# Expert stages of a two-layer block: order of the shared tile, output banks, routing by batch

## The reference

```python
# layer one: 8 experts, hidden width 128, and one shared expert without weight
scores = sigmoid(h @ gate_w.T); sel = top_k(scores + bias, 2)
routed += (silu((s*h) @ w1[e].T) * ((s*h) @ w3[e].T)) @ w2[e].T   # s: the chosen score
shared = (silu(h @ sw1.T) * (h @ sw3.T)) @ sw2.T
# layer two: 8 experts, hidden width 176, and one shared expert
p = softmax(h @ w_router); the two largest, divided by their sum, are the weights
out = sum_e weight_e * (silu(h @ w1[e]) @ w2[e]) + silu(h @ w_shared1) @ w_shared2
```

## Time and profile before

| what | value |
|---|---|
| median of 3 runs | 999.11 us |
| lowest and highest | 995.98 and 1001.66 us |
| the profiled execution | 992.07 us, of which the span is 990.3 us |
| mean granted PE clock in it | 0.939 of full |
| PE, DVE, ACT, POOL busy | 85%, 79%, 56%, 47% of the span |
| experts of layer one | about 618 to 725 us |
| heads of layer two | about 723 to 883 us |
| experts of layer two | about 889 to 985 us, the store behind it |

### The profile page before, as it was taken

The page is one execution under the profiler, slowest core; times in us unless marked ns, Lnnn a source line. Parts: engine busy times, 40 slices in busy tenths (PEclk is TensorE's granted clock), DMA queues, the critical chain, the costliest instruction groups (busy, mean ns, idle before and its releaser), DMA issues. The chain is left out here.

```text
span 990.3 us, 16625 instructions
## 1 busy us (share of the span) xinstructions
PE 844.1 (85%) x5407; PEld 596.8 (60%) x5486; DVE 780.0 (79%) x1734; ACT 553.9 (56%) x1222; POOL 466.5 (47%) x459
## 2 busy tenths in 40 slices
PE   5778899999999999999998899696966766847996
PEld 3456677767777777777776677353545424335564
DVE  6978999999999999999889997574689778583322
ACT  3758878777777877777766674011134552612111
POOL 2137676667776654554444445252222230602842
PEclk9979999999999999999999999799977887977898
DMA  7023333344333322214222223301115031022322
GB/s 255 27 65 106 135 113 105 125 133 134 112 133 127 94 85 83 79 65 128 87 86 65 86 65 141 131 23 65 47 47 89 1 51 16 1 91 74 113 68 73
DMA packets 52613, 87.15 MB, mean 88 GB/s; under 512 B 5784, under 2 KB 23704, under 8 KB 51760
## 3 DMA queue, kind: packets, MB, share of 16 engines
q1 hardware_dynamic: 43312, 73.50, 25.0%
q10 hardware_dynamic: 9216, 12.59, 3.4%
HBM read 70.67 MB, written 15.40 MB: 87 GB/s over the span
## 5 line engine op out<-in xcount | busy, mean ns | idle before, releaser
L580 PE MATMUL bank<-hTs,wA 128*128 128x512 bf16 x711 | 168.2, 382 | 3.7 <-DVE u L1813 0.5
L2343 POOL TENSOR_TENSOR xbuf<-xbuf,dec 128x384 f32<-128x384 f32 x64 | 53.5, 835 | 211.7 <-ACT xbuf L1294 169.6
L1813 DVE SCALAR_TENSOR_TENSOR u<-bank,chn,u 128x511 f32<-128x511 f32 (+2 forms) x192 | 142.9, 744 | 3.5
L580 PEld LDWEIGHTS bank<-hTs,wA 128*128 128x128 bf16 x768 | 75.5, 99 | 83.3 <-issue 4.8
L652 PE MATMUL bank<-wB,yb 128*128 128x256 f32 x512 | 121.1, 380 | 0.7 <-DVE acc L1769 0.7
L2425 POOL TENSOR_TENSOR hf<-hf 128x512 bf16<-128x512 f32 x44 | 47.5, 1080 | 116.6 <-DVE hf L2051 105.1
L580 PE MATMUL bank<-hTs,w 128*128 128x512 bf16 x354 | 89.9, 399 | 11.9 <-issue 9.4
L652 PEld LDWEIGHTS bank<-wB,yb 128*128 128x128 f32 x512 | 92.5, 190 | 11.1 <-issue 1.1
L2353 POOL TENSOR_TENSOR yb<-yv,gs 128x512 f32<-128x512 f32 x64 | 81.8, 1279 | 14.0 <-DVE yv L1840 13.8
L731 PE MATMUL bank<-Mm,xbuf 128*128 128x128 f32 x512 | 71.9, 285 | 18.8 <-DVE yv L1840 17.5
L731 PEld LDWEIGHTS bank<-Mm,xbuf 128*128 128x128 f32 x512 | 66.0, 196 | 30.2 <-issue 21.3
(11 more groups left out here) (258 smaller groups left out, 1826.1 us busy)
## 6 DMA issues: line engine op xcount, KB each, us to landing
csb<-csd SPq DMA_DIRECT2D x64, 256.0 KB, 3.5
wA<-in_win SPq DMA_DIRECT2D x32, 256.0 KB, 4.3
wAd<-wA ACTq DMA_DIRECT2D x32, 256.0 KB, 4.5
wA<-wAd SPq DMA_DIRECT2D x32, 256.0 KB, 3.8
sS<-cbd SPq DMA_DIRECT2D x24, 256.0 KB, 3.2
wB<-in_wob SPq DMA_DIRECT2D x8, 512.0 KB, 6.1
wBd<-wB ACTq DMA_DIRECT2D x32, 128.0 KB, 4.4
wB<-wBd SPq DMA_DIRECT2D x8, 512.0 KB, 5.4
```

The lines of the kernel that those rows point to most:

```text
L580: last = nc.tensor.matmul(out, wpart(a, kt), hpart(c, kt), start=n == 0, stop=n == 5)
L1813: nc.vector.scalar_tensor_tensor(out=u[:, n % 2, d:S], in0=bank[0][:, 0:S - d], scalar=chn[:, hid, 3 - d:4 - d], in1=u[:, n % 2, d:S], op0 ...
L2343: nc.gpsimd.tensor_tensor(Xw[:, n % 2, :].rearrange("p (t n) -> p t n", n=P), Xdt[:, n % 2, 0:S - P].rearrange("p (t n) -> p t n", n=P), d ...
```

## The change

- **Shared tile first.** In layer one, when tile m is shared, DVE does `hidden(m)` before `scaled(m + 1)` (at m = 0 also `gated_rows(1)` before it).
- **Turned weights and the copy.** For batch 0 of layer one PE turns the weights before `products(0)`, ACT copies them before its first `hidden`. SP issues `weight_rows(0, 0)` before the modulation weights. The pieces of work for batch 1 on PE, ACT and DVE move back by one step; the normalised rows are split from the roots and follow one step later.
- **Own output banks.** `OUT = ((6, 7), (4, 5))`: batch 0 adds up in banks 6 and 7, batch 1 in banks 4 and 5. The wait for `xf_done` goes.
- **Order of layer two.** Both shared tiles of batch 0 and then both of batch 1 come first, then batch 0's routed tiles, then batch 1's.
- **Routing by batch.** In layer two transposing, routing, split, exponent, normalising and choosing are done for batch 0, then for batch 1; the weights are turned after product 0 and after step 3. The clearing of `zerob` stands before the normalising.
- **End.** The wait for `a_x` goes. Batch 1's rows of layer two are gated and added in two halves; the store is three transfers, of batch 0 and of each half of batch 1.

The semaphores `d_wm0`, `d_wmr` and `d_wm1` become one, `d_wm`, and the early returns for `stop` go.

```diff
+        OUT = ((6, 7), (4, 5))
+        TILES = ([(b, pos) for b in range(B) for pos in range(FT[0])],
+                 [(b, pos) for b in range(B) for pos in range(SHARED[1])]
+                 + [(b, pos) for b in range(B) for pos in range(SHARED[1], FT[1])])
...
@@ SP
             sp.wait_ge(q["out_done"], TB * (N // HG))
+            weight_rows(0, 0)
             for kt in range(KT):
-                sp.dma_start(wm1[kt], io["wmod"][1, :, kt, :]).then_inc(q["d_wm1"], 16)
-            for b in range(B):
-                weight_rows(0, b, b + 1)
+                sp.dma_start(wm1[kt], io["wmod"][1, :, kt, :]).then_inc(q["d_wm"], 16)
+            weight_rows(0, 1)
...
-            weight_rows(1, 0, B)
-            sp.wait_ge(q["xf_done"], 2 * B)
-            store()
+            for b in range(B):
+                weight_rows(1, b)
+            sp.wait_ge(q["xf_done"], B + 1)
+            store(0, TB)
+            for half in range(2):
+                sp.wait_ge(q["xf_done"], B + 2 + half)
+                store(TB + 2 * half, TB + 2 * half + 2)
+            sp.wait_ge(q["d_out"], 48)
@@ PE, experts(L)
                 if L:
-                    transposed_rows(n0)
                     for b in range(B):
-                        routes(L, b, bank[6][:, b * TB * E:(b + 1) * TB * E])
+                        for ft in range(KT):
+                            turned_rows(n0, b, ft, bank[(2, 0)[b] + ft])
+                        routes(L, b, bank[4][:, b * TB * E:(b + 1) * TB * E])
...
-                pe.wait_ge(q["hts_done"], 6 if L == 0 else 12)
-                products(0)
                 if L == 0:
                     turned_weights(0, 0, bank[3])
+                    pe.wait_ge(q["hts_done"], 6)
+                    products(0)
                     pe.wait_ge(q["rg_step"], ROOT * (N // HG - 1) + 1)
                     out_product(TB - 1, N // HG - 1, bank[DRAIN[TB - 1]])
                     pe.wait_ge(q["cbT_done"], 1)
                 else:
-                    pe.wait_ge(q["rt_dve"], 1)
+                    pe.wait_ge(q["hts_done"], 10)
+                    products(0)
+                    turned_weights(1, 0, bank[1])
                 products(1)
...
-                        if m:
-                            pe.wait_ge(q["xf_done"], L * B + m // nf)
-                        for o in (6, 7):
+                        if L == 0 and b == 1:
+                            pe.wait_ge(q["cbT_done"], 2)
+                        if L and b == 1:
+                            pe.wait_ge(q["rt_dve"], 2)
+                        cleared(b)
                     rows_out(m)
-                    if L and m == 1:
-                        for b in range(B):
-                            turned_weights(1, b, bank[4 + b])
+                    if L and m == 3:
+                        turned_weights(1, 1, bank[3])
@@ DVE, experts(L)
                 else:
+                    nc.vector.memset(zerob[:], 0.0).then_inc(q["zb_done"], 1)
                     normalise(1, B)
...
+                    for b in range(B):
+                        less_largest(b)
+                        for ft in range(KT):
+                            split_part(n0, b, ft)
+                        shares(b)
...
                 for m in range(B * nf):
-                    if L == 0 and m + 1 < B * nf and tile(0, m + 1)[1] >= SHARED[0]:
+                    ahead = L == 0 and m + 1 < B * nf and tile(0, m + 1)[1] >= SHARED[0]
+                    shared = tile(L, m)[1] < SHARED[L]
+                    if ahead and not shared:
                         scaled(m + 1)
                     if L == 0:
                         first_batch(m)
                     hidden(m)
+                    if L == 0 and m == 0:
+                        gated_rows(1)
+                    if ahead and shared:
+                        scaled(m + 1)
                     if L == 0:
                         second_batch(m)
-                    if m > nf and m % nf == 1:
-                        add_experts(m // nf - 1)
-                add_experts(B - 1)
+                    if m == last_tile(L, 0) + 2:
+                        add_experts(0)
+                add_experts(1)
```

More of the change, by code:

```diff
@@ L284, in weighted @@
         def weighted(L, m):
-            b, pos, _ = tile(L, m)
-            return (B * (FT[0] - SHARED[0]) if L else 0) + b * (FT[L] - SHARED[L]) + max(0, pos + 1 - SHARED[L])
+            routed = sum(pos >= SHARED[L] for _, pos in TILES[L][:m + 1])
+            return (B * (FT[0] - SHARED[0]) if L else 0) + routed
         def hidden_tiles(L, m):
@@ L298, in spans @@
                     for e in range(E) if e * HID1 < (f + 1) * P and (e + 1) * HID1 > f * P]
-        weighted_tiles = [(L, m) for L in range(2) for m in range(B * FT[L]) if m % FT[L] >= SHARED[L]]
+        weighted_tiles = [(L, m) for L in range(2) for m in range(B * FT[L]) if TILES[L][m][1] >= SHARED[L]]
         def landed(j):
@@ L865, in experts @@
                 for m in range(B * nf):
+                    b, pos, _ = tile(L, m)
                     if m + 2 < B * nf:
-                        if L == 0 and m + 2 == nf:
-                            pe.wait_ge(q["hts_done"], 8)
+                        if tile(L, m + 2)[0:2] == (1, 0):
+                            pe.wait_ge(q["hts_done"], 8 if L == 0 else 12)
                         products(m + 2)
@@ L999, in heads @@
                 keys_queries(1)
-                pe.wait_ge(q["d_wm1"], 16 * KT)
+                pe.wait_ge(q["d_wm"], 32 + 16 * KT)
                 pe.wait_ge(q["scb_done"], 2)
@@ L2053, in add_experts, with gated, added @@
                 def add_experts(b):
-                    dve.wait_ge(q["fout"], tiles(L, nf * (b + 1) - 1))
-                    for m in range(2):
-                        last = nc.vector.tensor_tensor(xo[:, 2 * m:2 * m + 2, :],
-                                                       bank[6 + m][:, :].rearrange("p (t d) -> p t d", t=2),
+                    dve.wait_ge(q["fout"], tiles(L, last_tile(L, b)))
+                    def gated(m):
+                        return nc.vector.tensor_tensor(xo[:, 2 * m:2 * m + 2, :],
+                                                       bank[OUT[b][m]][:, :].rearrange("p (t d) -> p t d", t=2),
                                                        gm[:, L, 1, b, :].unsqueeze(1).to_broadcast([P, 2, D]), ALU.mult)
-                    link(last)
-                    part = slice(b * TB, (b + 1) * TB)
-                    nc.vector.tensor_tensor(x_sb[:, part, :], x_sb[:, part, :], xo[:], ALU.add).then_inc(q["xf_done"], 1)
+                    def added(t0, t1):
+                        part = slice(b * TB + t0, b * TB + t1)
+                        nc.vector.tensor_tensor(x_sb[:, part, :], x_sb[:, part, :], xo[:, t0:t1], ALU.add)\
+                            .then_inc(q["xf_done"], 1)
+                    if L and b:
+                        for m in range(2):
+                            link(gated(m))
+                            added(2 * m, 2 * m + 2)
+                        return
+                    gated(0)
+                    link(gated(1))
+                    added(0, TB)
                     dve.wait_ge(q["xf_done"], L * B + b + 1)
                 for m in range(B * nf):
-                    if L == 0 and m + 1 < B * nf and tile(0, m + 1)[1] >= SHARED[0]:
+                    ahead = L == 0 and m + 1 < B * nf and tile(0, m + 1)[1] >= SHARED[0]
+                    shared = tile(L, m)[1] < SHARED[L]
+                    if ahead and not shared:
                         scaled(m + 1)
@@ L2397, in low_halves, with input_rows @@
                 nf, own = FT[L], FT[L] - SHARED[L]
-                def input_rows(m):
-                    f = tile(L, m)[2]
-                    if m < SHARED[L]:
+                def input_rows(pos):
+                    f = (own + pos) % nf
+                    if pos < SHARED[L]:
                         pool.wait_ge(q["d_wa"], 32 * (L + 1))
@@ L2409, in input_rows, with output_rows @@
                         .then_inc(q["fw_done"], 1)
-                def output_rows(m):
-                    f = tile(L, m)[2]
-                    if m >= SHARED[L]:
+                def output_rows(pos):
+                    f = (own + pos) % nf
+                    if pos >= SHARED[L]:
                         pool.wait_ge(q["d_w2"], 32 * (L + 1))
@@ L2426, in hidden_rows @@
                         .then_inc(q["fhs_done"], 1)
-                for m in range(3):
-                    input_rows(m)
+                for pos in range(3):
+                    input_rows(pos)
                 for m in range(B * nf):
-                    if m < nf:
-                        output_rows(m)
+                    b, pos, _ = tile(L, m)
+                    if b == 0:
+                        output_rows(pos)
                     hidden_rows(m)
-                    if m + 3 < nf:
-                        input_rows(m + 3)
+                    if b == 0 and pos + 3 < nf:
```

(1 more changed line is left out.)

154 lines of the change are left out of this document (74 added, 80 removed).

## The result

The changed kernel takes 963.96 us (median of 4 runs, 961.88 to 964.57) against 997.88 us for the kernel before (4 runs, 995.98 to 1001.66): ratio 0.965, 95% interval 0.962 to 0.969. The forecast was 967, in 957 to 979.

A forecast was written before the change was run, and what follows sets the result against it. TensorE, the fullest engine, was taken as the bound, losing where it stands still or runs at lower clock. Gains 17.6 + 13.3 + 1.6 = 32.5 us, off the 999.11 median: 966.6, said as 967, range 957 to 979.

The forecast's parts named there:

- Layer one, opening and batch 0: Layer one's experts before the batch change: no idleness before product 2, rows out 2 at 640.4 against 650.45.
- Rival A: Layer one's batch 0: DVE becomes the bound, layer one gives 11 us, time 973 us; chance 0.17.
- Rival B: Layer one's opening: rows come no sooner, the copy's 5.5 us being its own; time 972 us; chance 0.07.
- Rival C: Layer two: the clock stays at 0.50; 1033 us if over all of it; chance 0.03.
- D: Better than forecast: clock stays up before layer two's batch 1 (16.5), roots take 2.2 us (18.6): 962 us; chance 0.13.
- Heads: The heads between the two layers' experts: only their start moves; 0, within 2 us each way.
- Batch change: Layer one, batch 0 to 1: 4.81 us of idleness for x_sb and about 1.5 us of half clock go.
- Layer two: Layer two's experts: less routing before product 0, no stall, no batch-change idleness; 13.3 us gained, 11 to 16.5.
- Tail: After the last update: a last store of 256 KB instead of 1 MB gains 1.6 us; 0 to 2.4.

The follow-up runs named there:

- changed_again: The changed kernel, unaltered, timed and profiled a second time: 960.47 us, ratio 0.964.
- one_bank_pair: The changed kernel with layer one's batch 1 adding up in banks 6 and 7 again, with PE's wait for x_sb: 966.79 us, 0.968.
- last_tile_and_rows_later: last_tile_first plus, at layer one's opening, batch 1's statistics and eight root steps one step later and cbT's copy before SP's wait: 962.63 us, 0.967.
- weights_before_copy: The changed kernel with SP issuing the modulation weights ahead of the copy of cbT and the rows again: 963.12 us, 0.967.
- batch_order: The changed kernel with layer two's old order of tiles, two shared tiles at the front of each batch: 964.78 us, 0.966.
- both_undone: The changed kernel with the edits of weighing_first and weights_before_copy together: 972.77 us, 0.976.
- late_turning_four: The changed kernel with layer two's batch 0 weights turned after step 1 again, four shared tiles still in front: 962.62 us, 0.968.
- last_tile_first: The changed kernel with DVE making hidden tile 17 before batch 0's normalised rows at layer one's last step: 960.20 us, 0.965.
- weighing_first: The changed kernel with DVE's old order in layer one, weighing the next tile ahead of the shared tile's product: 970.56 us, 0.973.

## Why the prediction was right

**The sum.** 32.5 us were forecast; the first profile shows 28.3 less, the second 32.4 less (990.3 against 957.9). Of the 4.1 us between these two, 3.3 are the clock in the scan's last matmuls. The medians give 33.9 (997.88 less 963.96), and in changed_again 36.6 (997.06 less 960.47). The profile of the kernel before, 992.07 us, is one of its faster executions (989.57 to 1004.40 in that run), so some 4 us of the larger median gain lie in no stage of the table, and where they belong stays open.

**Layer one, opening and batch 0.** The forecast had rows out 2 at 640.4, 22.4 us after the opening; it came after 22.5 and, again, 22.2. Each link was seen: the copy at once and its rows 1.5 us later (1.6 to 1.9 forecast), product 2 without a gap, waits of 1.88 and 2.00 us at rows out 1 and 2 (1.8 and 2.0 forecast). The root steps took 4.2 us beside GpSimd, as taken, the second of them 1.03 us.

**The term that was mis-sized**: 17.6 us for this stage, measured 16.2 and 16.7. The forecast let rows out 2 and product 5 run at full speed, 1.52 and 2.75 us. They took 2.10 and 3.87 in the first profile and 2.69 and 3.25 in the second, 1.7 us too much in each. PE's clock over them, behind the two waits:

```profile
644.40:650.10 5.70, 5.65 (x25) 2.98 (x26) 3.51 (x6) 0.00 (x0) 3.68 (x5) 0.70 0.15 54
...
```

0.70 here, and 0.70 in the second profile too (640.6 to 646.2). I had priced each wait by its own length and not the clock behind two waits close together. Against it, the forecast wait of 1.0 us at rows out 7 was 0.17 us, 0.8 too much in the forecast, and rows out 11 waited 0.40 us where none was forecast. The clock does not fall every time. Eight profiles have waits of 1.6 to 1.9 and of 2.0 us there and the clock fell behind the second in each; one_bank_pair has the same two waits and stayed at 1.00:

```profile
642.49 1.52 PE L851 MATMUL bank<-w,hf 128*128 128x256 bf16 x12 [1.99 <-POOL hf L2476]
...
```

```profile
642.40:646.40 4.00, 3.86 (x23) 2.40 (x25) 3.55 (x6) 0.00 (x0) 1.98 (x3) 1.00 0.08 27
...
```

From rows out 2 to rows out 3 it took 4.73 us there and 6.00 in changed_again. So the slow clock cost 1.3 us and not 1.7: at full clock PE waits 0.18 us at rows out 3 for a low half, which came late because one more size was off. The normalised rows took 3.12 us on DVE where 1.38 had stood in the trace before; in the second profile they ended at 642.34 and the low half of tile 3 was ready at 645.26, when PE at full clock would have asked for it at about 645.1.

The Trainium skill, "SBUF — State Buffer", section "SBUF: two separate sides", has DVE and GpSimd lock each other out where the DVE operation runs in a two-port mode, or has two SBUF inputs while the GpSimd operation reads SBUF. The forecast had weighed the second kind alone, and the root step of 1.03 us that it named as agreeing is itself a TENSOR_SCALAR with one input. The normalising operation has one wide input and two columns; which mode it ran in no trace here shows. GpSimd worked from 639.38 to 642.19 beside it. In the kernel before and in last_tile_and_rows_later GpSimd stood idle while the same four instructions ran (644.57 to 649.26 and 643.93 to 648.03), and both times they took 1.38 us. So the longer time goes with GpSimd's work; that the lock is the reason is argued, not shown.

**Rival A** (DVE as bound) did not come: from rows out 3 to rows out 15 PE's longest wait for a low half is 0.40 us. **Rival B** (the copy's time is its own) fell by weights_before_copy. **Rival C** (the clock stays low in layer two) did not come: PE's rows are at full clock from 891 us on. The three products of the opening still started slowly, though less so (6.07 us before; 883.59 to 889.84 less the turned weights' 0.86 is 5.4). **D** (clock up in layer two's opening, quick root steps) did not occur either: batch 1's 16 routing matmuls took 3.55 us where batch 0's took 1.92, and the roots 4.2.

**Heads.** 0 within 2 us was forecast; they were 0.4 us shorter and equal in the two profiles, but 3.4 longer in another kernel (batch_order) with the same heads (last section).

**Batch change.** 4.81 of waiting and about 1.5 of clock were forecast to go with the banks; one_bank_pair puts them at 6.9 us from rows out 8 to rows out 11. The remaining 1.0 of the 7.9 us there I put down to hidden tile 9 being early, which the schedule counted: product 11 had waited 1.63 us for it (680.99), and waits 2.73 in both_undone. The rows of weights for batch 1 cost PE no wait (cover of 3.5 us was forecast).

**Layer two.** 13.3 us forecast, 13.5 and 13.9 measured. Product 0 came 6.4 us after the normalised rows (6.5 forecast). The sum was right for a reason that was partly wrong: it named four shared tiles in front of the weighed ones as the cover of the stall, beside the early turning. The runs show two covers for one wait. The early turning alone leaves 0.2 us, within the spread (batch_order), the four tiles alone leave 1.1 us (late_turning_four), and without either it costs 9.2 us. Routing 3.1, the stall 9.2 and the batch change's 1.35 make 13.7 of the 13.9; the 1.35 was not tested by a run.

**Tail.** 1.6 us forecast, 2.1 measured, because 256 KB of store took 2.3 us, where the loads of that size had 2.7.

**Of the two reasons that I formed later** one fell, that the last wait of layer one was the normalised rows' (last_tile_first). The other, that DVE's order and the copy's order cost more undone together than singly, holds in the opening (7.5 against 6.1 us) and not over the stage (10.7 against 11.9), where the wait and the clock at the batch change differ from profile to profile.

## What to carry to other kernels

Walk the chain from a small result to its first user across every queue it passes: here the worst stalls were a 16 KB copy behind 1.5 MB that nobody needed yet, and a product behind a weighing whose data was late. Price a TensorE wait with the clock behind it, and as a range: 4.1 us of waiting brought a product to 4.4 us instead of 2.75, and two waits of about 2 us close together cost 1.3 us more in eight profiles and nothing in the ninth. When two edits cover the same wait, undo each alone and both: undoing one cost 1.1 us or 0.2, undoing both 9.2. When two edits are undone together, cut the stage where their waits lie: equal sums over a whole stage can hide unequal parts.

## What the runs showed of the hardware that was not expected

PE's granted clock stood near half through uninterrupted work: 0.57 over 8 us with PE busy for 8.00 of them, in three of the thirteen profiles of the changed kernel and its variants, and not in the one of the kernel before, at 3.3 us each time. Pauses came before: in the first profile PE idled 0.74 us before 610.30 and 0.16 before 612.43, at a clock of 1.00 until 614, and 0.62 from there to 616. changed_again has the same pauses, 0.74 and 0.17 us, and stayed at 1.00. The like stands in the scan, where in all fourteen profiles PE waits 2.56 or 2.57 us before the same 8 matmuls (between 563 and 571 us, L744 of the changed kernel): they took 1.13 us in six and 1.54 to 2.05 in eight. So the same pause is followed by either level of the clock. The heads, the same instructions in all these kernels, took between 156.73 us (weighing_first) and 161.38 us (batch_order), with PE's mean granted clock at 0.85 in the second profile of the changed kernel and 0.82 in batch_order:

```profile
706.75:864.77 158.02, 109.30 (x1007) 68.24 (x1005) 127.86 (x371) 73.76 (x139) 44.49 (x38) 0.85 0.16 31
...
```

```profile
709.12:870.50 161.38, 112.65 (x1006) 68.33 (x1005) 126.84 (x371) 73.65 (x139) 46.55 (x38) 0.82 0.16 30
...
```

What sets it there stays open; it is why a stage was compared with the same stage, and not a span with a span.
